# Lookup level one moved to GpSimd alone, and the last job's normalisation done tile by tile on VectorE, in a two-layer post-norm transformer kernel

## What is computed

```python
x = layernorm(x + attn0(x, Wq, Wk, Wv, Wo))        # 32 query heads, 8 key heads, head size 8
x = layernorm(x + ffn0(x, gate_w, up_w, down_w))   # weights rounded to fp8; 768 hidden; silu(gate) * up
x = layernorm(x + attn1(x, wq, wk, wv, wo))        # 16 query heads, 8 key heads, head size 16
x = layernorm(x + ffn1(x, lut, gate_idx, up_idx, down_idx))   # w = lut[idx], 16 values; 688 hidden
```

## Time and profile before

| | us |
|---|---|
| median of 3 runs | 363.53 |
| lowest, highest | 360.98, 364.22 |
| the profiled execution, its own time | 362.06 |
| its span, first to last instruction | 360.2 |

### The profile page before, as it was taken

How to read it: one execution, slowest core, us unless ns; L and a number is a source line. 1 busy time by engine, 2 the same in 40 slices (tenths; PEclk the granted TensorE clock), 3 DMA queues, 4 the chain that set the end, 5 groups by cost and what they waited for, 6 DMA issues and landing times.

```text
span 360.2 us, 7105 instructions
## 1 busy us (share of the span) xinstructions
PE 299.7 (83%) x2608; PEld 198.9 (55%) x2608; DVE 258.1 (72%) x399; ACT 246.3 (68%) x449; POOL 195.2 (54%) x261
## 2 busy tenths in 40 slices
PE   8446127687869897998979999999999999999990
PEld 7334002222426462564535765687778887979990
DVE  7695999898889897999986676656754657416341
ACT  3766677988588868797677776687677636654340
POOL 5756562404195348983398422564664346528763
PEclk9858555879899999999999999999999999999996
DMA  6468571201331000230001650032013000000000
GB/s 196 135 159 208 151 237 29 89 23 51 100 92 48 5 5 25 67 95 0 24 5 39 189 181 4 1 85 52 0 32 105 0 5 31 1 2 31 0 31 29
DMA packets 24872, 23.06 MB, mean 64 GB/s; under 512 B 3542, under 2 KB 24838, under 8 KB 24838
## 3 DMA queue, kind: packets, MB, share of 16 engines
q1 hardware_dynamic: 24838, 22.61, 22.2%
HBM read 10.47 MB, written 3.26 MB: 38 GB/s over the span
## 4 chain that ended last, share of the span: by engine, by line
PE 58%; DVE 13%; POOL 8%; ACT 8%; issue 7%; SPq 4%; DMA 2%; POOLq 0%; DVEq 0%; ACTq 0%
PE FB L1236 16%; PE PV L1179 9%; PE FB L1249 8%; PE MM L1124 6%; DVE LV L1042 5%; DVE MX L950 5%; PE SC L1158 4%; PE FB L1208 3%; PE SC L1153 2%; ACT PB L838 2%; PE FB L1078 2%; PE FB L1191 2%; SPq L542 2%; DMA QS<-QP 2%; ACT LV L885 2%
## 5 line engine op out<-in xcount | busy, mean ns | idle before, releaser
L950 DVE TENSOR_REDUCE MX<-MM 128x4 f32<-128x1024 f32 x96 | 117.0, 1219 | 40.1 <-PE MM L1124 39.5
L838 ACT ACTIVATE PB<-SC 128x1024 f32<-128x1024 f32 x96 | 98.2, 1023 | 31.7 <-PE SC L1153 19.5
L1124 PE MATMUL MM<-KS,QS 62*128 62x256 bf16 (+1 forms) x384 | 47.5, 292 | 33.6 <-DVE MX L950 24.8
L1179 PE MATMUL PV<-PB,VP 128*32 128x256 f32 x768 | 61.8, 408 | 1.3 <-ACT PB L838 1.3
L706 POOL TENSOR_TENSOR HL<-HF,HH 128x256 fp32r<-128x256 f32 (+1 forms) x48 | 37.6, 787 | 45.0 <-ACT HH L815 45.0
L1124 PEld LDWEIGHTS MM<-KS,QS 62*128 62x128 bf16 (+1 forms) x384 | 19.4, 97 | 59.4 <-DVE MX L950 39.4
L1042 DVE COPY_PREDICATED LV<-LB,LV 128x1728 f32<-128x1728 uint8 (+2 forms) x30 | 42.6, 1419 | 3.5 <-POOL LV L724 3.1
L1236 PE MATMUL FB<-XH,W 128*128 128x256 f32 x192 | 42.9, 305 | 0.5 <-DVE HF L1002 0.5
L1236 PE MATMUL FB<-XL,W 128*128 128x256 f32 x192 | 38.5, 282 | 0.0
L999 DVE SCALAR_TENSOR_TENSOR AA<-TH,FB 128x256 f32<-128x256 f32 (+1 forms) x48 | 20.0, 416 | 22.4 <-ACT TH L829 19.6
L1153 PE MATMUL SC<-QS,KS 64*128 64x256 bf16 x256 | 26.5, 287 | 9.8 <-ACT PB L838 7.8
(11 more groups left out here) (96 smaller groups left out, 578.5 us busy)
## 6 DMA issues: line engine op xcount, KB each, us to landing
QS<-QP SPq DMA_DIRECT2D x48, 128.0 KB, 2.4
IX<-in_idx SPq DMA_DIRECT2D x10, 216.0 KB, 4.0
dw<-LO SPq DMA_DIRECT2D x10, 216.0 KB, 2.1
W1L<-dw SPq DMA_DIRECT2D x10, 216.0 KB, 3.8
KS<-KP SPq DMA_DIRECT2D x24, 64.0 KB, 2.0
XT<-in_xt SPq DMA_DIRECT2D x4, 256.0 KB, 3.0
X<-in_x SPq DMA_DIRECT2D x4, 256.0 KB, 4.0
out<-X SPq DMA_DIRECT2D x4, 256.0 KB, 2.1
```

The source lines that it names most:

```text
L838: act.activation(PB[:, quad % PB_QUADS, kt, :, :], SC[:, :, :], ACT.Exp, scale=DH[layer(j)] ** -0.5).then_inc(exp_done, 1)
L950: dve.tensor_reduce(mx, MM[:, :, :].rearrange("p (f i) s -> p f i s", f=2), axis=AX.X, op=ALU.max).then_inc(max_red, 1)
L1124: ins = pe.matmul(MM[:, 2 * f + i, :], QS[lo:lo + r, j % NST, qs + h, qt * P:(qt + 1) * P], keys(j)[lo:lo + r, j % NST, ks, :], start=True ...
L1179: ins = pe.matmul(PV[32 * c:32 * c + 32, r % 2, :], v, PB[:, quad % PB_QUADS, kt, place(j, c), :], start=part == 0, stop=part == (3, 1)[la ...
```

## The change

1. GpSimd does all four parts of `lut1`; ScalarE's are gone, with their semaphore.
2. The mean is subtracted in one step (`ALU.subtract` with the mean itself), and `NM` is gone.
3. For job 7 the last norm is done per tile. The down matmuls write into `MM`, tile by tile within each of the six pieces; VectorE adds the sum from PSUM, takes the statistics, adds EPS; GpSimd takes only the power; VectorE scales (`fin`); each tile has its own output DMA.
4. All five order strings are written anew. (On TensorE the steps ahead of `score.4.0` are the same set as before.)

```diff
@@ POOL
                     n = norms[step]
+                    if step == ("down", JOBS - 1):
+                        for t in range(TT):
+                            pool.wait_ge(var_last, t + 1)
+                            pool.tensor_tensor(RSTD[:, n % 2, t:t + 1], VE[:, n % 2, t:t + 1], NHALF[:, 0:1],
+                                               ALU.pow).then_inc(rstd_last, 1)
+                        continue
                     pool.wait_ge(mv_done, n + 1)
-                    pool.tensor_scalar(NM[:, n % 2, :], MV[:, n % 2, :, 0], -1.0, 0.0, ALU.mult, ALU.add)
...
-                        ins = pool.tensor_scalar(X[:, batch(j), t, :], X[:, batch(j), t, :], NM[:, n % 2, t:t + 1],
-                                                 RSTD[:, n % 2, t:t + 1], ALU.add, ALU.mult)
+                        ins = pool.tensor_scalar(X[:, batch(j), t, :], X[:, batch(j), t, :],
+                                                 MV[:, n % 2, t, 0:1], RSTD[:, n % 2, t:t + 1], ALU.subtract, ALU.mult)
@@ ACT
-                elif kind == "lut1":
...
-                    for i in range(2 * part, 2 * part + 2):
-                        ins = act.activation(LV[:, i, :], LB[:, 0, :], ACT.Identity, scale=LD[:, i:i + 1],
-                                             bias=LT[:, 2 * i:2 * i + 1])
-                    ins.then_inc(level1_act, 1)
@@ DVE
+                    n = norms[step]
+                    dve.wait_ge(x_new, n - 1)
+                    for t in range(TT):
+                        dve.wait_ge(down_half, t + 1)
+                        link(dve.tensor_tensor(X[:, b, t, :], X[:, b, t, :], MM[:, 2 * t, :], ALU.add))
+                        link(dve.bn_stats(BST[:, n % 2, t, :], X[:, b, t, :]))
+                        link(dve.bn_aggr(MV[:, n % 2, t, :], BST[:, n % 2, t, :]))
+                        dve.tensor_scalar(VE[:, n % 2, t:t + 1], MV[:, n % 2, t, 1:2], 1.0, EPS, ALU.mult,
+                                          ALU.add).then_inc(var_last, 1)
+                elif kind == "fin":
...
+                    for t in range(TT):
+                        dve.wait_ge(rstd_last, t + 1)
+                        dve.tensor_scalar(X[:, b, t, :], X[:, b, t, :], MV[:, n % 2, t, 0:1], RSTD[:, n % 2, t:t + 1],
+                                          ALU.subtract, ALU.mult).then_inc(x_last, 1)
...
-                        dve.wait_ge(level1, 2 * (c + 1))
-                        dve.wait_ge(level1_act, 2 * (c + 1))
+                        dve.wait_ge(level1, 4 * (c + 1))
@@ PE
+                    if j == JOBS - 1:
+                        if i == 0:
+                            pe.wait_ge(max_red, unit0(JOBS))
+                        for t in range(TT):
+                            for k, (part, hs) in enumerate(products):
+                                ins = pe.matmul(MM[:, 2 * t, :], hs[0:rows(l, i), i, t * P:(t + 1) * P],
+                                                ffn_down(l, i)[part], start=i + k == 0,
+                                                stop=(i, k) == (5, len(products) - 1))
+                            if i == 5:
+                                ins.then_inc(down_half, 1)
+                        continue
@@ SP
+                    if j == JOBS - 1:
+                        for t in range(TT):
+                            sp.wait_ge(x_last, t + 1)
+                            sp.dma_start(out[batch(j), t * P:(t + 1) * P, :], X[:, batch(j), t, :]).then_inc(out_wr, 16)
+                        continue
```

The orders, cut to the pieces of which the prediction speaks. VectorE around chunk 5, and at the end of layer 0's maxima:

```diff
-        "max.1.8 max.1.9 lut2.4 max.1.10 lut3.4 turn.0.1 max.1.11 lut4.4 lutbits.5 max.1.12 max.1.13 wo.0 max.1.14 "
-        "lut2.5 max.1.15 lut3.5 mt.1.1 max.2.0 lut4.5 max.2.1 lutbits.6 gu.0.0 gu.0.1 max.2.2 max.2.3 gu.0.2 max.2.4 "
...
-        "mt.2.1 max.3.0 gu.1.0 max.3.1 gu.1.1 max.3.2 gu.1.2 max.3.3 lut2.8 max.3.4 gu.1.3 max.3.5 gu.1.4 max.3.6 "
-        "gu.1.5 turn.2.0 max.3.7 lut3.8 mt.3.0 max.3.8 lut4.8 lutbits.9 max.3.9 turn.2.1 max.3.10 max.3.11 down.1 "
-        "max.3.12 wo.2 max.3.13 lut2.9 max.3.14 lut3.9 max.3.15 lut4.9 mt.3.1 max.4.0 gu.2.0 max.4.1 gu.2.1 gu.2.2 "
-        "turn.3.0 max.4.2 gu.2.3 gu.2.4 max.4.3 gu.2.5 mt.4.0 max.4.4 max.4.5 max.4.6 max.4.7 mt.4.1 max.5.0 max.5.1 "
...
+        "max.1.10 lutbits.4 q8.11 max.1.11 max.1.12 turn.0.1 max.1.13 max.1.14 lut2.4 max.1.15 lut3.4 mt.1.1 lut4.4 "
+        "max.2.0 lutbits.5 max.2.1 wo.0 turn.1.0 max.2.2 max.2.3 max.2.4 lut2.5 lut3.5 lut4.5 gu.0.0 lutbits.6 gu.0.1 "
...
+        "gu.1.2 max.3.1 lut2.7 max.3.2 lut3.7 max.3.3 lut4.7 max.3.4 lutbits.8 max.3.5 gu.1.3 max.3.6 turn.2.0 "
+        "max.3.7 gu.1.4 mt.3.0 max.3.8 gu.1.5 lut2.8 max.3.9 lut3.8 max.3.10 turn.2.1 lut4.8 max.3.11 lutbits.9 "
+        "max.3.12 down.1 max.3.13 wo.2 max.3.14 max.3.15 mt.3.1 max.4.0 max.4.1 gu.2.0 max.4.2 gu.2.1 lut2.9 gu.2.2 "
+        "max.4.3 gu.2.3 mt.4.0 gu.2.4 max.4.4 gu.2.5 lut3.9 max.4.5 lut4.9 turn.3.0 max.4.6 max.4.7 down.2 mt.4.1 "
```

GpSimd around the same chunk:

```diff
-        "lut1.3.1 q8w.8 q8w.9 q8w.10 q8w.11 lutlow.3 lut1.4.0 lut1.4.1 kdif.3 kv.3 lutlow.4 xadd.0 lut1.5.0 lut1.5.1 "
-        "wo.0 xd.0 lutlow.5 lut1.6.0 lut1.6.1 hsplit.0.0 hsplit.0.1 hsplit.0.2 hsplit.0.3 hsplit.0.4 hsplit.0.5 "
...
+        "lutlow.3 q8w.11 lut1.4.0 lut1.4.1 kdif.3 lut1.4.2 lut1.4.3 kv.3 xadd.0 lutlow.4 lut1.5.0 lut1.5.1 wo.0 "
+        "lut1.5.2 lut1.5.3 xd.0 lutlow.5 hsplit.0.0 lut1.6.0 hsplit.0.1 lut1.6.1 hsplit.0.2 lut1.6.2 hsplit.0.3 "
```

More of the change, by code:

```diff
@@ L345, in two_layer_kernel @@
         MV = sb("MV", [P, 2, TT, 2])
-        NM = sb("NM", [P, 2, TT])
         RSTD = sb("RSTD", [P, 2, TT])
@@ L412, in two_layer_kernel @@
         x_new = sem("x_new")
+        x_last = sem("x_last")
+        var_last = sem("var_last")
+        rstd_last = sem("rstd_last")
+        down_half = sem("down_half")
         th_done = sem("th_done")
@@ L429, in two_layer_kernel @@
         level1 = sem("level1")
-        level1_act = sem("level1_act")
         lut_done = sem("lut_done")
@@ L611, in _ @@
                                  X[:, batch(j), :, :]).then_inc(out_wr, 16)
-            sp.wait_ge(out_wr, 16 * B)
+            sp.wait_ge(out_wr, 16 * (B + TT - 1))
         @block.gpsimd
@@ L875, in _ @@
                     act.activation(IB[:, :], IX[:, c % 2, :], ACT.Copy).then_inc(ib_done, 1)
-                elif kind == "lut1":
-                    _, c, part = step
-                    if c == 0 and part == 2:
-                        act.wait_ge(lut_steps, 1)
-                    act.wait_ge(bit_done, c + 1)
-                    if c >= 1:
-                        act.wait_ge(low_done, c)
-                    for i in range(2 * part, 2 * part + 2):
-                        ins = act.activation(LV[:, i, :], LB[:, 0, :], ACT.Identity, scale=LD[:, i:i + 1],
-                                             bias=LT[:, 2 * i:2 * i + 1])
-                    ins.then_inc(level1_act, 1)
                 elif kind == "lutlow":
@@ L987, in _ @@
                     b = batch(j)
-                    dve.wait_ge(x_sum, j + 1)
-                    layer_norm(b, step)
+                    if j < JOBS - 1:
+                        dve.wait_ge(x_sum, j + 1)
+                        layer_norm(b, step)
+                        continue
+                    n = norms[step]
[8 more added lines that the diff above has]
+                elif kind == "fin":
+                    b = batch(JOBS - 1)
+                    n = norms["down", JOBS - 1]
+                    for t in range(TT):
+                        dve.wait_ge(rstd_last, t + 1)
+                        dve.tensor_scalar(X[:, b, t, :], X[:, b, t, :], MV[:, n % 2, t, 0:1], RSTD[:, n % 2, t:t + 1],
+                                          ALU.subtract, ALU.mult).then_inc(x_last, 1)
                 elif kind == "gu":
```

## The result

The changed kernel is slower: median 369.23 us of 4 runs (367.84 to 370.20) against 363.29 us for the kernel before beside it, a ratio of 1.017 [1.0109, 1.0232], so 1.1 to 2.3% slower. The forecast was 357.1 us (351 to 363). The profiled execution took 367.84 us (span 366.1), the one before 362.06 (span 360.2).

What follows compares the result with a forecast made beforehand. Limits change by stage: VectorE leads a chain of three engines from 60 to 200 us, then TensorE is full. Terms -2.1 - 3.5 - 3.0 + 1.3 + 1.2 - 0.3 = -6.4 us from 363.53 gave 357.1 us, range 351 to 363.

Steps and rivals of the forecast that it cites:

- part 5: 15 norms without GpSimd's negation: each about 0.27 us shorter on the way to `tr`; -0.3 us, bounds 0 and -0.8.
- part 1: After the last matmul: last norm per tile, output DMA issued at 355.5 instead of 357.64; -2.1 us, bounds -1.5 and -2.7.
- Parts 2 and 3: Middle stage: ScalarE loses 40 level-one instructions, -3.5 us; new order moves VectorE work behind the maxima `score.4.0` needs, -3 us.
- rival A: ScalarE's relief is worth nothing, GpSimd's costs eat the order's gain, only the tail's stays: 361.4 us; chance 0.22.
- Part 4: GpSimd takes 40 more level-one instructions: late chunks +1.3 us and mutual blocking with VectorE +1.2 us.
- The term for chunks that come late: VectorE waits at `lut2` for level one in five early chunks; +1.3 us, bounds 0 and 10.
- The port's term: VectorE's fp8 copies, bit masks and `mt` steps delayed beside GpSimd's level one; +1.2 us, bounds 0 and 5.
- B: Level one on GpSimd alone sets the middle stage's pace, VectorE waiting at `lut2`: 368 to 372 us; chance 0.1.
- The mark of the forecast: From 60 to 200 us TensorE's wait for exponentials falls from 7.8 us to 4 or so.
- C: The relief works fully, all 7.8 and 4.7 us come through, GpSimd hides its own: 349 us; chance 0.08.

Runs made afterwards that it cites:

- experiment 1: Changed kernel with one edit undone: GpSimd negates the mean again and adds it; 359.33 us, 0.9911 of the kernel before.
- 3: Kernel before with only the last job's sums and norm done tile by tile, its orders otherwise untouched; 359.08 us, 0.9923.
- 7: Changed kernel with the mean negated again and level one's parts 2 and 3 left out from chunk 1 on, made by nobody; 355.83 us, 0.9816.
- 6: Kernel before with the new tail and ScalarE's half of level one left out from chunk 1 on, made by nobody; 359.73 us, 0.9943.
- experiment 8: Changed kernel with the mean negated again and level one's parts 2 and 3 back on ScalarE, behind chosen exponentials; 373.88 us, 1.031.
- 5: Kernel before's order with the new tail and all of level one on GpSimd, the mean negated and added; 383.66 us, 1.0583.
- 4: Changed kernel with `add` in place of `subtract` in GpSimd's scaling, same operands, so the output changes; 358.13 us in one execution.

## Why the prediction was wrong

**The step that failed is part 5,** "15 norms each lose about 0.27 us ... I take -0.3", with bounds of 0 and -0.8. It counted the instruction that goes and took the one that stays as unchanged, since its size was. It measured +9.4 us (experiment 1 against the changed kernel; +13.7 in the kernel before). The duration of GpSimd's `add, mult` stood in the trace; that of `subtract, mult` did not, and it needed bounds from both sides, as part 1 gave them for VectorE's scaling, which the trace didn't show either. Thirty instructions with 0.69 us more each (1263 against 576) are 20.7 us of GpSimd; a bound of 0 to +20 would have moved the chances, if not the forecast.

**Part 1, the tail:** -2.1 forecast, -2.8 (-1.8 to -3.8) measured in 3. Mechanism and the 3.5 us (3.4) were right. VectorE's instructions came out at 0.42, 0.43, 0.18 and 0.15 where 0.42, 0.38, 0.125 and 0.19 stood.

**Parts 2 and 3, relief and order:** -6.5 forecast as two independent terms. Measured -3.9 together, in 7 against 3, with GpSimd's price left out. Relief alone is worth nothing that can be told (6), as rival A says, so what is gained needs the new order. Which part of the 3.9 the order would give without relief is what experiment 8 failed to settle. The 4.3 to 4.7 us of VectorE's work that moved behind `mt.3.0` and `mt.4.0` would fit a start of `score.4.0` that is 4.3 us earlier (215.9 against 220.2); that this is its cause is argued, not shown. With level one on GpSimd the gain is gone again: 221.1 in 1, and 223.8 in the changed kernel.

**Part 4, GpSimd's price:** +2.5 forecast (+1.3 late, +1.2 port), +3.4 measured, 7 against 1. The total was near and the split was not. The term for chunks that come late, +1.3, should have been nothing: the wait for level one is 2.8 us, where the kernel before had 3.1 for GpSimd. The port's term was priced on the wrong instructions, the fp8 copies, bit masks and `mt` steps. It is right that level one of a chunk can't meet the predicated copies of the same chunk. But GpSimd's later steps can: in experiment 1 chunk 7's copy took 4.44 us instead of 2.10, and ten copies together 3.6 us more than in 7. How much of the 3.4 us this is stays open. The Trainium skill's rule that a VectorE instruction with two SBUF inputs and a GpSimd read exclude each other ("SBUF — State Buffer", Who interferes with whom) agrees with the trace again: the copy of 4.45 us in the changed kernel ends at 161.75, 2.0 us after the third GpSimd instruction beside it (159.76), which is its own length without company, and the fourth, with a median of 0.67 us, took 2.29 and ended after it.

**The sum,** in parts of the time before: -0.77% tail, -1.07% order and relief, +0.95% GpSimd's price, +2.59% subtraction; that is +1.7%, the ratio measured, as it must be since each is the difference of two neighbours. Without part 5 it is -0.89%, 3.2 us faster, against a forecast of 6.1 without it. Of these 3.2 us the tail has 2.8: the move of level one and the new order cancel to -0.4 us, which is inside the noise (experiment 1, 0.9911, against 3, 0.9923). So parts 2 to 4, forecast at -4.0 us, came to nothing that can be told.

**The rivals.** B gave 368 to 372 us and the result is 369.2, but not by B's mechanism, whose mark (a wait for level one over 10 us) is absent; it would have been right for the old order, at 24 us (5). The mark of A, 20 us of idle TensorE from 60 to 200, appeared (26.4, and 22.8 without the subtraction), and its core, relief worth nothing, is shown in the old order. Its account, that GpSimd's costs eat part 3 and the tail alone stays, is the one that experiment 1 bears out. The mark of the forecast, fewer waits for exponentials, appeared only in part: 7.8 to 6.5. The chances had a slip besides: 0.6, most of C's 0.08 and a fifth of A's 0.22 are about 0.71 for faster by over 1%, not 0.68.

## What to carry to other kernels

Give every instruction whose operation changes a price of its own, even if its size and operands stay; in GpSimd's `tensor_scalar`, negate a small column and `add` rather than subtract on a wide tile. An engine that is idle a third of the time (GpSimd after the change) can still be on the chain: count what is queued behind its longest burst, a norm that nobody awaits included. Moving work to an engine that shares a port can be paid in waits (experiment 5) and in the durations of the other engine's instructions (experiment 7); the second shows in no wait, so compare durations by form before and after, the longest as well as the mean.

## What the runs showed of the hardware

- GpSimd's `tensor_scalar` on 128x256 float32: `add, mult` has a median of 558 ns with either operand for the mean (experiments 1 and 4; 576 and 585 on the mean), `subtract, mult` and `mult, subtract` 1223 ns (1263 on the mean). In the kernel before's order the means are 693 and 1443 ns. VectorE's `subtract, mult` of the same size: 0.41 us.
- A VectorE bit operation of 128x96, with one SBUF input, 0.20 us in the median of 12, took 2.04 us when GpSimd had started an instruction before it (the timeline of experiment 1):

```profile
28.75 1.03 POOL L655 TENSOR_TENSOR KP<-KR,KP 64x256 bf16<-64x256 f32 x1
...
29.18 2.04 DVE L1042 TENSOR_SCALAR BIG<-AA 128x96 int32<-128x96 int32 x1
...
29.77 1.39 POOL L742 TENSOR_SCALAR LV<-LB,LD,LT 128x432 f32<-128x432 uint8 x2
```

It ended at 31.22, with GpSimd's level one (29.77 + 1.39 = 31.16) and not with the instruction that was running when it began (29.78), as if it had let both pass. The copy that starts at 157.30 in the changed kernel looks the same, with three instructions ahead of it. No run isolates this.
